# Layer-3 pooling of a graph network: spreading the scores by a product with the identity, taking node rows to rank order tile by tile, and scaling them on ScalarE

## What is computed

```python
for i in range(DEPTH):                      # DEPTH = 3, RATIOS = (0.5, 0.5, 0.5)
    xs.append(x)
    h = jax.nn.relu(_sage_layer(x, x, src, dst, emask, dWl1[i], dWr1[i], db1[i]))
    x = _sage_layer(h, h, src, dst, emask, dWl2[i], dWr2[i], db2[i])
    w_ = pool_w[i]
    score = jnp.tanh(x @ w_ / jnp.linalg.norm(w_))
    k = int(math.ceil(RATIOS[i] * n))
    vals, perm = jax.lax.top_k(score, k)
    x = x[perm] * vals[:, None]
```

## Time and profile before

| | |
|---|---|
| time, median of 3 runs | 1106.29 us (1094.54 to 1112.35) |
| the profiled execution, its own time | 1097.9 us |
| its span, first to last instruction | 1096.1 us |
| TensorE busy | 971.7 us, 89% of the span |
| VectorE busy | 505.5 us, 46% |
| ScalarE busy | 243.8 us, 22% |
| GpSimd busy | 120.2 us, 11% |
| chain that ended last, by engine | TensorE 66%, VectorE 18%, transfers 6% |
| mean granted clock of TensorE | 0.952 of full speed |
| graph network of layer 3 | about 785 to 976 us of the span |

### The profile page before, as it was taken

One profiled execution on the slowest core, in us unless ns is written; L12 is line 12 of the kernel. 1 busy time (PEld: TensorE's weight loads), 2 busy tenths in 40 slices (PEclk: granted clock), 3 DMA queues, 4 the chain that ended last, 5 costly groups with the idle time before them and its releaser, 6 DMA issues.

```text
span 1096.1 us, 15443 instructions
## 1 busy us (share of the span) xinstructions
PE 971.7 (89%) x5696; PEld 798.7 (73%) x5696; DVE 505.5 (46%) x1530; ACT 243.8 (22%) x514; POOL 120.2 (11%) x125
## 2 busy tenths in 40 slices
PE   2899889789999989889997889999999988899896
PEld 1789655689999966689876768777877554566785
DVE  4667679652222241342258997522344152331222
ACT  0000012012222111413335764223010111024010
POOL 1000000012221110015410000000101000000241
PEclk9899899989999989989998999999999998799998
DMA  8200000028888430228642000154100000220762
GB/s 272 116 0 1 1 0 1 10 68 306 308 332 308 134 158 5 111 72 297 209 143 81 1 1 1 58 177 150 48 1 1 0 1 0 115 116 27 241 243 72
DMA packets 25928, 114.74 MB, mean 105 GB/s; under 512 B 5002, under 2 KB 8880, under 8 KB 18572
## 3 DMA queue, kind: packets, MB, share of 16 engines
q1 hardware_dynamic: 20297, 97.11, 24.9%
q0 software_dynamic: 5568, 16.78, 4.6%
HBM read 102.07 MB, written 11.81 MB: 104 GB/s over the span
## 4 chain that ended last, share of the span: by engine, by line
PE 66%; DVE 18%; DMA 6%; issue 5%; ACT 2%; POOL 1%; SPq 1%; DVEq 1%; POOLq 0%; ACTq 0%
PE PS L676 7%; PE PS L401 5%; PE PS L510 5%; PE PS L414 4%; PE PS L691 4%; PE PS L734 4%; PE PS L1055 4%; PE PS L720 3%; PE PS L472 3%; PE PS L378 3%; DVE arena L1728 2%; PE PS L756 2%; PE PS L804 2%; DVE ring L1703 2%; DMA arena<-flat_rows,route 2%
## 5 line engine op out<-in xcount | busy, mean ns | idle before, releaser
L378 PE MATMUL PS<-const 128*128 128x128 f32 x882 | 113.3, 290 | 7.8 <-DVE X L1122 2.1
L378 PEld LDWEIGHTS PS<-const 128*128 128x128 f32 x882 | 109.4, 204 | 11.7 <-issue 5.0
L676 PEld LDWEIGHTS PS<-HT,ring 128*128 128x128 f32 x680 | 78.4, 192 | 3.4 <-issue 2.6
L676 PE MATMUL PS<-HT,ring 128*128 128x128 f32 x680 | 78.8, 275 | 2.2 <-DVE HT L1623 1.3
L2263 POOL DMA_INDIRECT slot_rows<-ST,route x46 | 46.5, 1011 | 168.5 <-ACT ST L2035 99.6
L1620 DVE TENSOR_TENSOR HT<-HT,PS 128x256 f32<-128x256 f32 (+1 forms) x51 | 19.2, 376 | 93.6 <-ACT HT L2024 73.6
L510 PE MATMUL PS<-HT 125*125 125x250 bf16 x480 | 58.7, 289 | 3.5 <-DVE HT L1500 3.5
L2229 POOL TENSOR_TENSOR col<-col,power 125x5 f32<-125x5 f32 x9 | 10.6, 1179 | 462.9 <-DVE col L1137 363.5
L510 PEld LDWEIGHTS PS<-HT 125*125 125x125 bf16 x480 | 57.5, 148 | 4.6 <-DVE HT L1500 4.6
L878 PE MATMUL PS<-arena,HT 125*33 125x125 f32 x400 | 52.4, 279 | 0.0
L691 PE MATMUL PS<-ring,HT 128*128 128x256 f32 x204 | 46.7, 379 | 0.0
(11 more groups left out here) (407 smaller groups left out, 1718.4 us busy)
## 6 DMA issues: line engine op xcount, KB each, us to landing
ring<-in_experts SPq DMA_DIRECT2D x17, 1386.0 KB
ring<-in_experts SPq DMA_DIRECT2D x17, 768.0 KB, 5.7
ring<-in_experts SPq DMA_DIRECT2D x11, 1026.0 KB
arena<-in_experts SPq DMA_DIRECT2D x6, 1026.0 KB
ring<-in_experts SPq DMA_DIRECT2D x6, 1024.0 KB, 8.4
arena<-in_experts SPq DMA_DIRECT2D x6, 1024.0 KB
arena<-in_gnn SPq DMA_DIRECT2D x5, 1024.0 KB, 5.8
ring<-in_experts SPq DMA_DIRECT2D x8, 513.0 KB, 3.7
```

The source lines that it names most:

```text
L378: pe.matmul(PS[:, bank, 0:128], ident, ident, start=True, stop=True)
L676: mm = pe.matmul(PS[:, bank, at:at + SLOTS], both[:, j, k, m * 128:(m + 1) * 128], xs[0][i % 2][:, k, :], start=(k == 0), stop=(k == KD - 1))
```

## The change

The diagonals, the scaling on VectorE and the copy of the spread scores are taken out. TensorE spreads the scores by a product whose weights are one tile's score column, read 125 times over, and whose moving operand is the identity; the result stays in PSUM (banks 6 and 7 from column 0 of bank 6), where VectorE reads it as it counts. As a row of 625 crosses a bank at column 512, the fifth tile of level 0 is spread in two products. ScalarE scales the node rows, a tile at a time, with `root_scaled` counting them. VectorE adds up a tile's rank as soon as its counts are there, writes that tile of `PT` and signals it. TensorE takes the node tiles in the outer loop: for each it waits for its scaled rows and its part of `PT` and adds its share to all kept tiles, which lie in halves of bank 4 and in bank 5. A product of zeros opens and another closes the sums in bank 4 where there is more than one kept tile. One semaphore, `pooled_full`, tells VectorE that all is there. Some root products are issued ahead of the spreading and some behind it, the keep-busy products are fewer (2, 4 and 13 ahead of the spreading; 2, 2 and 6 behind it), and TensorE waits for the pooled copies before it starts the next level. `tanh_scores` is rearranged.

```diff
-        diag_ready, perm_ready, cmt_cleared = sem("diag_ready"), sem("perm_ready"), sem("cmt_cleared")
+        score_ready, perm_ready, cmt_cleared = sem("score_ready"), sem("perm_ready"), sem("cmt_cleared")
+        score_rows, root_scaled, pooled_full = sem("score_rows"), sem("root_scaled"), sem("pooled_full")
...
-        scoreb = scratch[:, 0:N]
+        score_at = 6 * 512
+        scoreb = PF[0:TP, score_at:score_at + N]
+        pooled_tiles = [sum(len(tiles(LEVELS[j])) for j in range(i + 1)) for i in range(3)]
...
+                    early = (3, 2, 0)[i]
+                    for t, c0, c in ts[:early]:
+                        root_tile(act_bank(), xt, gw(f"ur1_{i}"), c0, c).then_inc(act_full, 1)
+                    pe.wait_ge(dve_free, n["v"])
+                    stay_busy(4, (2, 4, 13)[i])
+                    pe.wait_ge(score_ready, i + 1)
+                    score = col[:, 168:168 + NT]
+                    for t, c0, c in ts:
+                        for a, b in ((c0, min(c0 + c, 512)), (max(c0, 512), c0 + c)):
+                            if b > a:
+                                mm = pe.matmul(PF[0:TP, score_at + a:score_at + b], score[0:c, t:t + 1].broadcast_to([c, TP]),
+                                               ident[0:c, a - c0:b - c0], start=True, stop=True)
+                    mm.then_inc(score_rows, 1)
                     if i < 2:
-                        for t, c0, c in ts:
+                        for t, c0, c in ts[early:]:
                             root_tile(act_bank(), xt, gw(f"ur1_{i}"), c0, c).then_inc(act_full, 1)
-
-                    emptied()
-                    if i == 2:
-                        stay_busy(4 + n["v"] % 4, 13)
-                    pe.wait_ge(diag_ready, i + 1)
...
-                    for kt, k0, kc in ks:
-                        bank = dve_bank()
-                        if kt == 0:
-                            stay_busy(bank, (36, 17, 9)[i])
-                            pe.wait_ge(perm_ready, i + 1)
-                        for t, c0, c in ts:
-                            mm = pe.matmul(PS[0:kc, bank, 0:D], PT[0:c, t, k0:k0 + kc], ROOT[0:c, t, :],
-                                           start=(t == 0), stop=(t == len(ts) - 1))
-                        mm.then_inc(dve_full, 1)
+                    for t, c0, c in ts:
+                        if t == 0:
+                            stay_busy(4, (2, 2, 6)[i])
+                            if len(ks) > 1:
+                                pe.matmul(PS[0:TP, 4, :], zeros[:, 0:TP], zeros[:, :], start=True, stop=False)
+                        pe.wait_ge(root_scaled, pooled_tiles[i] - len(ts) + t + 1)
+                        pe.wait_ge(perm_ready, pooled_tiles[i] - len(ts) + t + 1)
+                        for kt, k0, kc in ks:
+                            mm = pe.matmul(PS[0:kc, 4 + kt // 2, kt % 2 * D:(kt % 2 + 1) * D], PT[0:c, t, k0:k0 + kc],
+                                           ROOT[0:c, t, :], start=(t == 0 and (kt == 2 or len(ks) == 1)),
+                                           stop=(t == len(ts) - 1 and (kt == 2 or len(ks) == 1)))
+                    if len(ks) > 1:
+                        mm = pe.matmul(PS[0:TP, 4, :], zeros[:, 0:TP], zeros[:, :], start=False, stop=True)
+                    mm.then_inc(pooled_full, 1)
...
+                        pe.wait_ge(xn_ready, n["xn"] + len(ks))
...
-                link(dve.tensor_scalar(sign, s, 0.0, 2.0, ALU.is_ge, ALU.mult))
-                link(dve.tensor_scalar(sign, sign, -1.0, None, ALU.add))
+                link(dve.tensor_scalar(half, s, 0.0, -0.5, ALU.is_ge, ALU.add))
                 dve.wait_ge(tanh_in_read, level + 1)
-
-                link(dve.scalar_tensor_tensor(sign, mask, 0.0, sign, ALU.is_equal, ALU.mult))
+                link(dve.scalar_tensor_tensor(half, mask, 0.0, half, ALU.is_equal, ALU.mult))
+                dve.wait_ge(tanh_out, 2 * level + 1)
+                link(dve.tensor_tensor(small, small, mask, ALU.mult))
+                link(dve.scalar_tensor_tensor(small, half, -2.0, small, ALU.mult, ALU.add))
                 dve.wait_ge(tanh_out, 2 * (level + 1))
-                dve.tensor_tensor(small, small, mask, ALU.mult)
                 link(dve.tensor_scalar(big, big, 1.0, None, ALU.add))
                 link(dve.reciprocal(s, big))
-                link(dve.tensor_scalar(s, s, 2.0, -1.0, ALU.mult, ALU.add))
-                link(dve.tensor_tensor(s, s, sign, ALU.mult))
-                link(dve.tensor_tensor(s, s, small, ALU.add))
+                link(dve.scalar_tensor_tensor(s, s, 4.0, half, ALU.mult, ALU.mult))
+                dve.tensor_tensor(s, s, small, ALU.add).then_inc(score_ready, 1)
...
-                    for t, c0, c in ts:
-                        ins = dve.tensor_scalar(diag[:, t, :], ident[0:TP, 0:TP], score[:, t:t + 1], None, ALU.mult)
-                    ins.then_inc(diag_ready, 1)
-                    for t, c0, c in ts:
-                        ins = dve.tensor_scalar(ROOT[0:c, t, :], ROOT[0:c, t, :], score[0:c, t:t + 1], None, ALU.mult)
-                    link(ins)
...
-                            taken(dve.tensor_copy(scoreb[:, c0:c1], PS[0:TP, b, 0:c1 - c0]))
-                    own_banks()
-
-                    link(dve.memset(tie[0], 0.0))
+                    dve.wait_ge(score_ready, i + 1)
+                    dve.wait_ge(score_rows, i + 1)
...
+                        own = rank[0:c, t:t + 1]
+                        if c0:
+                            link(dve.scalar_tensor_tensor(own, own, tie[0][0:c, t:t + 1], tie[1][0:c, t:t + 1],
+                                                          ALU.add, ALU.add))
+                        else:
+                            link(dve.tensor_tensor(own, own, tie[1][0:c, t:t + 1], ALU.add))
+                        dve.tensor_scalar(PT[0:c, t, 0:kept], CONST(const, "iota", TP)[0:c, 0:kept], own, None,
+                                          ALU.is_equal).then_inc(perm_ready, 1)
+                    dve.wait_ge(pooled_full, i + 1)
...
+                    act.wait_ge(score_ready, i + 1)
+                    for t, c0, c in tiles(rows_):
+                        act.activation(ROOT[0:c, t, :], ROOT[0:c, t, :], ACT.Identity,
+                                       scale=col[0:c, 168 + t:169 + t]).then_inc(root_scaled, 1)
...
-                pool.wait_ge(perm_ready, i + 1)
+                pool.wait_ge(perm_ready, pooled_tiles[i])
```

More of the change, by code:

```diff
@@ L1791, in tanh_scores @@
             def tanh_scores(s, level):
-                small, big, sign, mask = (col[:, 208 + 8 * j:208 + 8 * j + NT] for j in range(4))
+                small, big, half, mask = (col[:, 208 + 8 * j:208 + 8 * j + NT] for j in range(4))
                 dve.scalar_tensor_tensor(big, s, -1.0, s, ALU.mult, ALU.max).then_inc(tanh_in, 1)
@@ L1861, in layer3_gnn @@
                                                       accum_out=tie[1][0:c, t:t + 1]))
[L1862 to L1871 removed]
+                        own = rank[0:c, t:t + 1]
[7 more added lines that the diff above has]
+                    dve.wait_ge(pooled_full, i + 1)
                     for kt, k0, kc in ks:
[L1873 to L1875 removed]
+                        ins = dve.tensor_copy(XL[i + 1][0:kc, kt, :], PS[0:kc, 4 + kt // 2, kt % 2 * D:(kt % 2 + 1) * D])
                         if i < 2:
[L1877 removed]
+                            ins.then_inc(xn_ready, 1)
                 dve.memset(CMT, 0.0).then_inc(cmt_cleared, 1)
```

27 lines of the change are left out of this document (removed).

## The result

The changed kernel took 1087.5 us (median of four runs, 1087.0 to 1088.3), the kernel before 1103.9 (four runs, 1094.5 to 1112.4): a ratio of 0.9851, 95% interval 0.9806 to 0.9897. That is faster by 1.5%, inside the 2% that the forecast called no change; the forecast was 1092.3. The profiled run took 1088.3 (span 1086.5, mean granted clock 0.949).

What follows compares the result with a forecast made beforehand. The bound was taken to be the chain that ended last, two thirds TensorE and 18% VectorE. Levels 0, 1 and 2 save 9.3 + 3.5 + 1.2 = 14.0 us: 1097.9 becomes 1083.9, plus 8.4 for the median, 1092.3; range 1079 to 1103.

Steps and rivals of the forecast that it cites:

- (a): Level 0 score chain: as many links as before, one unlinked operation (0.08 us) gone; scores final at 820.1.
- (b): Level 0, no diagonals and fewer root tiles first: spreading product starts with the scores at 820.15, not 821.67.
- (c): Level 0 spreading product: 12 records instead of 10, 1.5 us instead of 1.24; ranks can start at 821.6.
- (d): Level 0: no copy, tie-column clearing or wait (1.04 us before); with the earlier steps, ranks start 2.3 us earlier.
- (e): Level 0 ranking: 8.95 us as before, last permutation tile at 830.6, tile 0 at 823.3, each further one 1.8 later.
- (f): Level 0 scaling on ScalarE: five of 0.45 us, 2.3 in all, always ahead of the ranks, costing nothing by itself.
- (g): Level 0 pooling tail: last tile's products 830.6 to 831.9, zero product 0.29; next product at 832.2, 9.3 us earlier.
- The unknown costs: Counting from PSUM (27 instructions, 1.6 us either way) and repeated-column weights (up to 4.4 us), both taken as 0.
- A: Rival: the clock falls in the new pooling; level 0 saves 4.0 instead of 9.3, 8.7 in all: 1097.6; chance 0.13.
- B: Rival: PSUM reads and repeated weights cost their upper ends, 1.6 and 4.4 us; 8.0 saved: 1098.3; chance 0.08.
- C: Rival: clock stays low behind the pooling too, through L955's 50 records, 13.4 us more; 4.7 slower: 1111; chance 0.03.
- D: Rival: level 2 keeps its clock (2.6 us) and PSUM reads cost their lower end (1.6); 18.2 saved: 1088.1; chance 0.08.

Runs made afterwards that it cites:

- no_busy: The changed kernel without any keep-busy products between the last aggregation-weight product and the pooling, at all three levels; 1092.3 us, run once.
- one_signal: The changed kernel with every pooling product waiting for all of its level's permutation tiles; 1110.6 us, ratio 1.0045 to the kernel before.
- gaps: The changed kernel with six more keep-busy products, in two gaps around the transposes of level 2; 1090.5 us, run once.

## Why the prediction was right, point by point

**The whole.** Fourteen us were forecast for the three levels and 12.6 came. Taken back one at a time, the parts are: overlap 9.5, diagonals 1.8, copy 1.65, scaling −0.3. The 11.8 ± 1.4 us between all runs agree with the 12.6.

```
us               level 0  level 1  level 2
overlap            6.52     2.35     0.59
diagonals          1.00     0.62     0.17
copy               0.84     0.48     0.33
scaling           -0.11    -0.10    -0.08
sum                8.25     3.35     1.01
measured           8.06     3.17     1.40
```

That the parts sum to 12.6 is in part chance: by level they miss by 0.2 to 0.4, in both directions. The overlap was taken back in the new order of products with the clock kept up, where the 30 records take 8.13 us; the kernel before ran its own order in 8.57, ten of the records at the low clock. And the runs for scaling and diagonals both contain the 0.1 by which the first count comes sooner, so the scaling is worth nothing rather than −0.3, and the diagonals 1.95. Read straight from the two traces, before less after, each stretch splits without a remainder:

```
us                                     level 0  level 1  level 2
last row to spreading product             1.32     1.00     0.23
product to first count                    0.58     0.61     0.57
first count to last permutation tile     -0.29    -0.06     0.05
last permutation tile to the end          6.45     1.62     0.53
```

The last line holds the overlap and, at level 0, the 1.9 us of low clock that the kernel before met. I had forecast 7.0 for it, of which two for the clock.

**(a) and (b), scores and start of the product: right, but for 0.2.** From the last row to the final scores took 3.39 us, before 3.26: L1812 stood 0.28 behind L1810 instead of following it, at level 0 alone (why stays open); at levels 1 and 2 the scores came after 3.11 instead of 3.20 and 3.19. TensorE was ready and started with the scores at all levels but level 2, where the keep-busy records held it as forecast.

**(c), the start of counting: right, 0.2 short.** Twelve records took 0.13 each, not 0.14, but VectorE started 0.14 behind their end: 1.70 instead of 1.5. **(d)** copy gone: confirmed.

**(e), the ranking: 0.26 short.** 9.21 us instead of 8.95. The adds, now one by one inside the chain, take longer than five together: 0.37 from the start of a tile's last accumulator read to its permutation tile (828.81 to 829.18).

**(f), the scaling: right.** Five took 2.10, ahead of everything that waits; the estimate of 0.45 each was near the measured 0.493. That they cost nothing is shown; that VectorE would have done them for nothing as well, and 0.1 better, I hadn't said.

**(g), the tail behind the ranking: the largest miss, 0.5 us.** I took 6 × 0.22 for a node tile and 0.29 for the zero product. The tile took 1.61, the zero product 0.35 (836.91 to 837.27, where 0.29 was 512/250 of a shorter one), and the start 0.15. The mis-sized term is the record: 0.216 holds only while the weight tile keeps its shape. The kernel before changed it once in 30 records, since its output tile was the outer loop; the new order changes it nine times. I counted records and not what the new loop order does between them. Only the last tile's share shows. The slack of 0.5 us a tile that I named shrank to 0.23 (1.87 less 1.64): TensorE has almost become the bound. Four tiles of it just sufficed to make up the 0.8 us by which the pooling began late.

The misses of level 0 are 0.2 + 0.2 + 0.26 + 0.5 = 1.2, and 9.3 − 8.06 is 1.24.

**Levels 1 and 2.** 3.17 for 3.5: the tail took 1.64 instead of 1.3 and the ranking 0.06 more, while counting started 0.1 earlier than forecast. 1.40 for 1.2: the keep-busy records held the product as I wrote, but it came 0.23 nearer to the last row than before, where I had put nothing.

**The unknown costs.** Both were taken at nothing and both are nothing: counts 870 and 731 ns from PSUM, 866 and 726 from SBUF; spreading 1.56 either way. The Trainium skill (VectorE: DVE Perf Modes, The TRN2 errata) puts 62 cycles more on a PSUM source; neither this pair nor the 8.79 against 8.83 shows them.

**The rivals.** A (the clock falls in the pooling) didn't come, and no_busy beside one_signal shows that the overlap itself prevents it at levels 0 and 1: with it the clock stayed even without keep-busy products, without it the clock fell in spite of them. B fell with both its prices. C's mechanism exists: in one_signal the clock stayed low for 20.5 us, through products with gaps of under 0.4. My argument against it, that the low stretch at 833 ended under continuous products, was therefore no protection; what kept C away is, as far as these runs show, that the change leaves no idle time such as the 2.45 us ahead of that stretch. D's first half, that level 2 keeps its clock once everything has shifted, happened in no profile of after. How long the low stretch lasts does differ from run to run (6.8, 3.4 and 6.8 us in the three); gaps shows that it hangs on missing work in two gaps of under 0.4 us. D's other half was nothing.

**The forecast of the median.** I added 8.4 us because the three runs shown had a median above the profiled run. Over all runs before averages 1104.8 and after 1093.0, so 1092.3 is close, but in part by luck: the 1106.3 that I started from was 1.5 above that average, and the 14.0 that I took off 2.2 above the difference of the averages (1.4 above the stretches).

## What to carry to other kernels

When a wait for a whole result becomes a wait for its tiles, the gain is what the consumer took, less the last tile with all that it needs: price that one exactly, with the loop order inside it. Before moving work off an engine, look whether that engine waits at this place anyway; if it does, the move is worth nothing. And small idle gaps ahead of a long row of products can cost more (up to 2.7 us here) than the gaps themselves.

## What the runs showed of the hardware

- A change of the weight tile between 125x125 and 125x63 delays the next record by 0.09 us and the one behind it by 0.05 to 0.10, at full clock.
- The granted clock fell while TensorE stood idle for 6.7 us (one_signal, 0.66 in 838 to 840) and 3.3 us (no_busy), and behind an idle time of 2.45 us (one_signal, 0.50 from 910.3 to 930.8, and not back sooner though products ran). It also fell in level 2 with no gap above 0.6 us; 12 records of keep-busy work, six in each of two gaps, were enough to hold it there.
- Over the runs of both kernels whose clock is listed the time falls by 7.5 us for each 0.01 of mean granted clock, and at equal clock the kernels differ by 10.6 us. Most of the scatter, and so the difficulty of measuring 1%, goes with the clock.
